# First expert stage with element 0's tokens gathered by expert, its combines beside the first retention, and weight splits over six attention pairs

## The reference, cut to what matters

```
x = x + 0.5 * ffn(layernorm(x))          # ternary weights, 1024 hidden
x = x + attention(layernorm(x))          # 16 heads of 128, rotary
x = x + 0.5 * ffn(layernorm(x))
x = x + 0.5 * moe(layernorm(x))          # first expert stage
x = x + retention(layernorm(x))
x = x + 0.5 * moe(layernorm(x))          # last expert stage

def moe(x):      # 8 experts of width 128, top 2 of softmax + bias, weights = the scores
    dw = zeros; dw[token, idx] += scores[token, idx]
    y = sum over e of dw[:, e] * ((silu(x @ W1[e].T) * (x @ W3[e].T)) @ W2[e].T)
    z = (silu(x @ Ws1.T) * (x @ Ws3.T)) @ Ws2.T      # shared expert, all tokens
    return y + z

def retention(x):
    q, k, v = xpos(x @ W_Q), xpos(x @ W_K, downscale=True), x @ W_V
    return ((q @ k.T) * decay) @ v
```

## Time and profile before

| | us |
|---|---|
| median of 3 runs | 1617.28 (1615.24 to 1617.81) |
| the profiled execution | 1616.08 |
| its span, first to last instruction | 1614.2 |
| mean granted TensorE clock | 0.997 |
| busy: TensorE, VectorE, ScalarE, GpSimd | 96%, 78%, 75%, 73% |
| first expert stage, first up to last down | 1253.1 to 1400.7 |
| last expert stage | 1491.3 to 1610.0 |

### The profile page before, as it was taken

The page is one execution under the profiler, slowest core; times in us unless marked ns, Lnnn a source line. Parts: engine busy times, 40 slices in busy tenths (PEclk is TensorE's granted clock), DMA queues, the critical chain, the costliest instruction groups (busy, mean ns, idle before and its releaser), DMA issues. The chain is left out here.

```text
span 1614.2 us, 26791 instructions
## 1 busy us (share of the span) xinstructions
PE 1556.4 (96%) x9211; PEld 904.0 (56%) x9211; DVE 1264.2 (78%) x2323; ACT 1213.3 (75%) x1904; POOL 1172.3 (73%) x823
## 2 busy tenths in 40 slices
PE   3998899999999999999999999999999999999898
PEld 2565445555555555545555555555567556688575
DVE  7888787777777777778888888778887776988628
ACT  7876888989989989888998999887665443345442
POOL 0865888888888888788888888888576322476635
PEclk9999999999999999999999999999999999999999
DMA  9312779899889888878899989977650000000532
GB/s 310 128 53 49 135 144 164 151 164 176 157 169 176 145 164 171 141 151 171 173 168 188 173 166 161 161 134 139 121 139 1 21 1 1 1 1 7 106 103 94
DMA packets 644101, 200.84 MB, mean 124 GB/s; under 512 B 601848, under 2 KB 641792, under 8 KB 643712
## 3 DMA queue, kind: packets, MB, share of 16 engines
q1 hardware_dynamic: 639392, 191.92, 60.8%
q0 software_dynamic: 1536, 4.20, 0.8%
q10 hardware_dynamic: 3040, 3.02, 0.5%
HBM read 36.91 MB, written 13.76 MB: 31 GB/s over the span
## 5 line engine op out<-in xcount | busy, mean ns | idle before, releaser
L993 POOL TENSOR_TENSOR Pl<-Pm,Ph 128x1024 f16<-128x1024 f32 x256 | 548.5, 2143 | 44.9 <-ACT Ph L1334 44.4
L1324 ACT ACTIVATE Pm<-banks,nbias,s_scale 128x1024 f32<-128x1024 f32 x256 | 307.4, 1201 | 95.7 <-DVE nbias L1953 95.3
L1951 DVE TENSOR_REDUCE nmax<-banks 128x1 f32<-128x1024 f32 x256 | 311.6, 1217 | 80.0 <-PE banks L2523 79.4
L1334 ACT ACTIVATE Ph<-Pm 128x1024 f16<-128x1024 f32 x256 | 268.1, 1047 | 1.5
L972 POOL TENSOR_TENSOR rp_b<-rp_s,rope 128x512 f32<-128x512 f32 x128 | 163.4, 1277 | 99.6 <-ACT rp_s L1301 98.0
L2521 PE MATMUL banks<-QK_hi 128*128 128x512 f16 x512 | 194.6, 380 | 2.2 <-DVE QK_lo L2051 1.6
L2522 PE MATMUL banks<-QK_lo,QK_hi 128*128 128x512 f16 x512 | 194.5, 380 | 0.0
L2523 PE MATMUL banks<-QK_hi,QK_lo 128*128 128x512 f16 x512 | 194.3, 379 | 0.0
L2523 PE MATMUL banks<-PT_hi,V_lo 128*128 128x512 f16 x512 | 194.0, 379 | 0.0
L2522 PE MATMUL banks<-PT_lo,V_hi 128*128 128x512 f16 x512 | 194.0, 379 | 0.0
L2521 PE MATMUL banks<-PT_hi,V_hi 128*128 128x512 f16 x512 | 194.0, 379 | 0.0
(11 more groups left out here) (312 smaller groups left out, 3983.8 us busy)
## 6 DMA issues: line engine op xcount, KB each, us to landing
moe_raw<-in_L_ffn_W SPq DMA_DIRECT2D x48, 128.0 KB, 2.9
w_all<-in_L_attn_w_qkv SPq DMA_DIRECT2D x3, 2048.0 KB, 15.8
a_raw<-in_L_attn_w_qkv SPq DMA_DIRECT2D x24, 256.0 KB, 3.2
PT_hi<-Ph SPq DMA_TRANSPOSE x256, 3.4
PT_lo<-Pl SPq DMA_TRANSPOSE x256, 3.4
w_rows<-m SPq DMA_DIRECT2D x9, 384.0 KB, 3.0
xs<-zeros SPq DMA_DIRECT2D x1, 2944.0 KB, 16.8
yd<-y_sb ACTq DMA_DIRECT2D x5, 512.0 KB, 2.9
```

What stands on the lines that cost most here:

```text
L993: nc.gpsimd.tensor_tensor(Pl[:, z % 4, :], Pm[:, k, :], Ph[:, z % 4, :], ALU.subtract).then_inc(pl_done.sem, 1)
L1324: nc.scalar.activation(Pm[:, k, :], two_banks[z % 2][:], ACT.Exp, bias=nbias[:, z:z + 1], scale=s_scale[:], accum_out=rsum[:, z:z + 1]).th ...
L1334: nc.scalar.activation(Ph[:, z % 4, :], Pm[:, (base * SLOTS + z) % 3, :], copy).then_inc(ph_done.sem, 1)
L1951: nc.vector.tensor_reduce(nmax[:, z:z + 1], two_banks[z % 2][:], AX, ALU.max, negate=True).then_inc(max_done.sem, 1)
```

## The change

The first expert stage gets the units of the last one, in an order of its own: shared units of element 0, shared half 0 of element 1, experts 0 and 1 on half 0 of element 1, the other shared half, six more dense units, the six gathered units (12 to 17), eight dense ones. 26 units in place of 36. Element 0's logits move into the FFN's end, its ranks and positions into the stage's beginning, scatter behind units 1 to 7, gathers behind units 20 to 25. Tiles 0 to 3 are combined behind units 22 and 23; tiles 4, 5 and 6, 7 on VectorE behind rotation groups 0 and 1 of the retention, whose second half is normalised and transposed only behind values 0 to 3. Helpers of the last stage take the stage number m and serve both. In attention the nine splits go to slots 9, 7 and 9, 9, 7 and 9, 9, 7 and 9 of pairs 9 to 14, and the scales' steps to slots 5, 8, 10 and 12 of pair 8, the rest to the second FFN.

Constants and attention:

```diff
+    FIRST_HALVES = [("d", DENSE, 0, 0), ("d", DENSE, 0, 1)]
+    FIRST_AHEAD = 8
+    UNITS = [SHARED[SORTED] + SHARED[DENSE][:1] + FIRST_HALVES + SHARED[DENSE][1:] + FIRST_ROUTED[2:FIRST_AHEAD] + TILES + FIRST_ROUTED[FIRST_AHEAD:],
+             SHARED[SORTED] + SHARED[DENSE] + ROUTED[:3] + TILES + ROUTED[3:]]
+    SCATTER_BEHIND = [{1: (0,), 2: (1, 2), **{t: (t,) for t in range(3, TT)}}, {0: (2,), 1: (3, 4), 2: (5, 6), 3: (7,)}]
+    GATHER_BEHIND = [{20: (0, 1), 21: (2, 3), 22: (4,), 23: (5,), 24: (6,), 25: (7,)},
+                     {15: (0, 1), 16: (2, 3), **{13 + t: (t,) for t in range(4, TT)}}]
+    FIRST_COMBINE_AT = {22: (0, 1), 23: (2, 3)}
+    RET_WEIGHTS_AT = (13, 15, 17)
+    FIRST_LOAD = 7
-    EXPERT_PAIRS, EXPERT_SLOTS = (9, 13), (9, 13)
+    EXPERT_SLOTS = {9: (9,), 10: (7, 9), 11: (9,), 12: (7, 9), 13: (9,), 14: (7, 9)}
```

VectorE in the second FFN and in pair 8:

```diff
+                    if f and phase == 2 and ht == 2:
+                        late_scales()
...
                 add(len(PHASES) - 2, 3)
+                if f:
+                    ln_variance(1, l + 1, 0)
...
                 mean_squares(len(PHASES) - 1)
+                if f:
+                    last_shifted(0, SORTED)
                 for j in range(TPH):
                     add(len(PHASES) - 1, j)
...
-                    if base == SCALE_PAIR and s == 7:
+                    if base == SCALE_PAIR and s == 5:
                         late_norm_maximum()
+                    if base == SCALE_PAIR and s == 8:
+                        late_norm_guarded()
+                    if base == SCALE_PAIR and s == 10:
+                        late_power()
                     if base == SCALE_PAIR and s == 12:
-                        late_scales()
+                        late_inverse()
```

TensorE (in the FFN, `if f and j == 2: router_logits(0, SORTED)` behind down 2):

```diff
+                unit_up(0, 0, experts_of)
+                unit_up(0, 1, experts_of)
+                rank_tokens(0)
+                turn(0)
+                unit_up(0, 2, experts_of)
+                unit_down(0, 0, experts_of)
+                unit_up(0, 3, experts_of)
+                turn(1)
+                unit_down(0, 1, experts_of)
+                for i in range(4, NUB):
+                    unit_up(0, i, experts_of)
+                    if i == 4:
+                        router_logits(0, DENSE)
+                    if i == FIRST_LOAD:
+                        experts_of += load_experts(0)
+                    unit_down(0, i - DOWN_LAG, experts_of)
+                for c in range(DC):
+                    if c:
+                        pe.wait_ge(mo_h_ready.sem, mo_h_ready.in_head(0, NUB - 1))
+                    transpose_part(0, l + 1, 0, c, bank[NEXT_TURN_BANK[c]])
+                for n in range(NUB - DOWN_LAG, NUB):
+                    unit_down(0, n, experts_of)
...
                 if b == 0:
-                    pe.wait_ge(x_added.sem, x_added.before(b, l) - 4)
+                    pe.wait_ge(x_added.sem, x_added.before(b, l))
                 for t in range(TPH):
                     values_of(t)
+                if b == 0:
+                    pe.wait_ge(r_vlo.sem, r_vlo.at(b, 2))
+                    transpose_x(0, l, 1, 4)
                 rotation(b, (2,))
```

VectorE's first expert stage, new (`combined_tiles` is `combine` and `ln_statistics` for each tile):

```diff
+                ln_variance(1, l, 1)
+                shifts(1, l, 0)
+                last_scores(0, SORTED)
+                last_pick(0, SORTED)
+                unit_product(0, 0)
+                last_second(0, SORTED)
+                shifts(1, l, 1)
+                unit_product(0, 1)
+                positions(0, SORTED)
+                norm_lo(0)
+                unit_product(0, 2)
+                choice_weights(0, SORTED)
+                unit_add(0, 0)
+                unit_product(0, 3)
+                norm_lo(1)
+                unit_add(0, 1)
+                for i in range(4, NUB):
+                    if i > DOWN_LAG + 2 and i != 6:
+                        unit_add(0, i - DOWN_LAG - 1)
+                    if i == 5:
+                        last_shifted(0, DENSE)
+                    if i == 6:
+                        last_scores(0, DENSE)
+                        last_pick(0, DENSE)
+                    unit_product(0, i)
+                    if i == 6:
+                        last_weights(0, DENSE)
+                        unit_add(0, i - DOWN_LAG - 1)
+                    if i in RET_WEIGHTS_AT:
+                        retention_weights_lo(RET_WEIGHTS_AT.index(i))
+                    combined_tiles(FIRST_COMBINE_AT.get(i, ()))
+                    if i == 23:
+                        ln_variance(0, l + 1, 0)
+                    if i == 24:
+                        shifts(0, l + 1, 0)
+                unit_add(0, NUB - DOWN_LAG - 1)
+                for c in range(DC):
+                    ln_lo_part(0, l + 1, 0, c, bank[NEXT_TURN_BANK[c]])
+                for n in range(NUB - DOWN_LAG, NUB):
+                    unit_add(0, n)
+                rotation(0, (0,))
+                combined_tiles((4, 5))
+                rotation(0, (1,))
+                combined_tiles((6, 7))
+                ln_variance(0, l + 1, 1)
```

GpSimd (`rows_lower(0, 0)` also behind step 6 of the FFN's last phase) and ScalarE:

```diff
+                rows_lower(0, 1)
+                rsqrt_ln(1, l, 1)
+                pool.wait_ge(xs_zero.sem, 16)
+                for i in range(NUB):
+                    expert_lo(0, i)
+                    if i == 1:
+                        rows_placed(0)
+                    if i == 24:
+                        rsqrt_ln(0, l + 1, 0)
+                    scatter(0, SCATTER_BEHIND[0].get(i, ()))
+                    gather(0, GATHER_BEHIND[0].get(i, ()))
+                rotation(0, (0,))
+                rsqrt_ln(0, l + 1, 1)
+                rotation(0, (1,))
...
+                for i in range(4, NUB):
+                    copy_out(0, i - DOWN_LAG - 1)
+                    unit_silu(0, i)
+                    unit_hi(0, i)
+                    if i == 5:
+                        router_exponential(0, DENSE)
+                    if i in RET_WEIGHTS_AT:
+                        retention_weights_hi(RET_WEIGHTS_AT.index(i))
+                    if i == NUB - 2:
+                        normalise(0, l + 1, 0)
...
                 if b == 0:
                     rotation(b, (1,))
+                    normalise(0, l, 1)
+                    ln_hi(0, l, 1, 4)
```

More of the change, by code:

```diff
@@ L394, in build_program, with combined, last_of, added_by @@
     LOGITS, RANKS = slice(D, D + TT * NE), slice(D + TT * NE, D + (2 * TT + 1) * NE)
[L396 to L416, removed]
+    N_SORTED = N_BEST + N_SECOND + N_POSITIONS + N_CHOICE
+    def combined(m, k, t):
+        return m * TOPK * TT + TOPK * t + k + 1
+    def last_of(m, b, half):
+        return max(i for i, u in enumerate(UNITS[m]) if u[0] != "x" and u[1:3] == (b, half))
+    def added_by(m, n):
+        return x_added.before(0, MOE_STAGES[m]) + 4 * sum(u[0] != "x" for u in UNITS[m][:n + 1])
+    def routed(m, b, step):
+        return m * (N_SORTED + N_BEST + N_WEIGHT) + b * N_SORTED + step
+    def lo_of_unit(m, i):
+        return lo_pool.sem, m * NUB + i + 1
+    def width(m, i):
+        kind, _, g, _ = UNITS[m][i]
         return GROUP_TILES[g] * P if kind == "x" else HALF
@@ L2215, in done @@
                     ins.then_inc(router_step.sem, 1)
-                    dve.wait_ge(router_step.sem, routed(b, step[0]))
+                    dve.wait_ge(router_step.sem, routed(m, b, step[0]))
                 return done
@@ new lines, in first_experts, with norm_lo, combined_tiles @@
+            def first_experts(l):
+                def norm_lo(half):
+                    for c in range(DC):
+                        ln_lo_part(1, l, half, c, bank[FIRST_TURN_BANK[half][c]])
+                def combined_tiles(tiles):
+                    for t in tiles:
+                        combine(0, t)
+                        ln_statistics(0, l + 1, t)
+                ln_variance(1, l, 1)
[34 more added lines that the diff above has]
+                unit_add(0, NUB - DOWN_LAG - 1)
+                for c in range(DC):
+                    ln_lo_part(0, l + 1, 0, c, bank[NEXT_TURN_BANK[c]])
[6 more added lines that the diff above has]
+                ln_variance(0, l + 1, 1)
@@ L2369, in last_experts @@
                     if i == WEIGHTS_AT:
-                        last_weights(1)
-                    product(i)
+                        last_weights(1, DENSE)
+                    unit_product(1, i)
                     if i == 1:
@@ L2381, in last_experts @@
                     for t in COMBINE_AT.get(i, ()):
-                        combine(t)
+                        combine(1, t)
                 for n in range(NUB - DOWN_LAG - 1, NUB):
-                    add(n)
+                    unit_add(1, n)
             def retention_weights_lo(part):
@@ new lines, in _, with load_experts @@
+            tile_registers = [nc.tensor.alloc_register(f"expert{j}") for j in range(SLOT_TILES)]
+            def load_experts(m):
+                pe.wait_ge(router_step.sem, routed(m, SORTED, N_BEST + N_SECOND + N_POSITIONS))
```

(3 more changed lines are left out.)

797 lines of the change are left out of this document (295 added, 502 removed).

## The result

The changed kernel takes 1626.4 us (median of four runs, 1624.7 to 1628.9) where the kernel before takes 1617.5 (median of four): the ratio is 1.0060, 95% interval 1.0048 to 1.0072. It is slower by some 9 us, beyond the 0.2% that can be told from no change. Forecast was 1621, own range 1615 to 1627, with slower as the likeliest outcome. The profiled execution took 1625.1 us, its span is 1623.3, so it stands 9.0 above the one profiled before.

The account below looks back on a forecast made before the run. The prediction took TensorE, busy 96% of the span, as the bound; work removed and stops added summed to +3.7 us on the profiled 1616.1, giving 1619.8, or 1621 against the runs' median; range 1603 to 1630, the forecast's own 1615 to 1627.

Parts of the forecast that it names:

- Work removed: First expert stage on TensorE: six gathered units replace element 0's 16 routed units; gain 31.9 us.
- 1, FFN tail: End of the FFN: TensorE's squares wait behind GpSimd's subtraction put ahead of the last sum of squares; +1.1 us.
- 3, positions: Before unit 2: TensorE waits for the low parts that stand behind positions; +4.1 us (2.5 to 5.5).
- 5, registers: Loading 23 registers on TensorE's queue, partly covered by up 7; +1.7 us (0.5 to 2.2).
- 6, scatter: 16 indirect DMAs behind units 1 to 7, done before TensorE comes to unit 12; 0 us.
- 7, stage end: From up 20's end to rotation group 0: gathers, combines, variance and normalisation hold down 22 and unit 25; +8.7 us (6 to 11).
- 8, entry: Rotation group 0 to group 2: rotations, combines and variance queue on VectorE before normalisation; +12.5 us (10 to 14).
- 9, clock: Half-clock stretches behind longer TensorE stops, two drops taken; +3.3 us (0 to 6.6).
- Attention: Parting pair 8's scales and moving splits to even pairs removes TensorE stops; -3.7 us (-5 to -1).
- first rival: VectorE not behind at rotation group 0, short combines, overlapping waits, no clock drop there; 1606 us, chance 0.28.
- The second: Rival that GpSimd's indirect DMAs and the idle clock cost more: slower combines, positions, two more drops; 1629 us, chance 0.18.
- The third: Rival that spreading splits over six pairs buys nothing, l_inv still stopping TensorE; 1625 us, chance 0.09.

Follow-up runs that it names:

- e6: Changed kernel with VectorE's add of unit 21 put ahead of the combines of tiles 2 and 3 and the first half's variance; 1.0057 of the kernel before.
- e2: Changed kernel with rotation group 1's VectorE work behind the second half's shifts, and ScalarE normalising before it rounds group 1's sums; 1.0032 of the kernel before.
- e5: Changed kernel with 48 more matmuls of 128x512, sums never read, on TensorE in the entry's 12.05 us stop; 1.0051 of the kernel before.
- e12: Changed kernel without its attention part: weight splits and late scales as in the kernel before; 1.0078 of the kernel before.
- e11: Changed kernel with reordered stage end and entry, earlier router, other split slots, and element 1's first low parts ahead of shifts and positions; 0.9933 of the kernel before.
- e3: Changed kernel with rotation group 1's work later at the entry and combines 4 and 5 moved into VectorE's pause behind product 24; 1.0019 of the kernel before.
- e8: Changed kernel with entry reordered, combines 4 and 5 and element 1's router earlier, unit 21's add ahead, even-pair splits in slots 9 and 13; 0.9966 of the kernel before.

## Why the prediction came out

The list of stops held, each at its place and behind the engine named; three sizes did not: clock, entry and attention. The sum was +3.7 on the profiled execution, +9.0 came. By its steps:

- **Work removed.** 33.7 us, not 31.9: the six gathered units took 28.7, my lower bound of 28.8, since nothing before them dropped the clock as in the earlier trace rows. The agreement that I claimed with 81 ns per pair was that of a sum which held half-clock time: here, at full clock, the pairs began 0.06 us apart in unit 12 and 0.08 to 0.09 in units 15 to 17.
- **1, FFN tail.** A stop of 0.84 us where I had 1.1. **2, ranks.** 3.48 for 3.6. **3, positions.** Transposes' start to unit 2 is 4.71 us, less 0.87 of work 3.8 for 4.1. **4, router.** 5.30 for 5.0.
- **5, registers.** Nothing: up 7's end and down 5 touch. The 2.2 us of the earlier trace rows are wholly covered by a full queue. Wrong by 1.7.
- **6, scatter.** 0, as said; the last of it was issued at 1306.6, unit 12 came at 1319.2.
- **7, stage end.** End of up 20 is 1358.00, so E = U + 34.1 where I had 33.0. The wait within down 22 was 4.57 for 3.1. e6 shows that moving this stop gains little, 1.5 us of this stretch in its trace and nothing clear in its time; the chain through combines and normalisation sets E, which is how I had added it up. The stretches at half clock show the same. From the end of this stop to E it is 12.27 us in the change, e2, e5 and e12, though up 25 between them took 4.94, 4.28, 3.38 and 3.30 us; e12's lines of the stop, of the start of down 23 and of E:

```profile
1380.00 0.39 PE L2448 MATMUL banks<-w,bT_hi 128*128 128x256 f16 x1 [4.51 <-DVE X L2224]
...
1384.55 0.27 PE L2448 MATMUL banks<-w,bT_hi 128*128 128x256 f16 x1
...
1392.27 0.38 PE L2448 MATMUL banks<-x,r_hi 128*128 128x512 f16 x1
```

- **8, entry.** 24.2 us for 21.2. The 12.06 us in front of the transposes was expected as "some 12". The transposes ran 2.71 us and 1.42 followed. VectorE ended the variance at E + 16.3 where I had 13.8. Nearly all of that is combines 4 and 5, 4.84 us for my 2.7; rotations and combines 6 and 7 took what I had. The first combine after rotation 0 took 2.53 us for its two operations, the one at 1404.75 0.99.

GpSimd's timeline beside that combine shows what ran at its side:

```profile
1397.63 2.84 POOL L1057 TENSOR_TENSOR rq_lo<-rot,rq_hi 128x512 fp32r<-128x512 f32 x2
...
1408.55 1.05 POOL L905 TENSOR_TENSOR rstd<-ve,small 128x4 f32<-128x4 f32 x1 [8.08 <-DVE ve L1640]
```

The two low parts lie over the drawn-out combines at 1396.81 and 1399.72, which took 2.53 and 1.55 us; between 1400.5 and 1408.5 GpSimd is idle, and each pair of operations took 0.99. The Trainium skill (SBUF — State Buffer, section SBUF: two separate sides) describes VectorE and GpSimd as blocking each other for a whole instruction on a port they share; the trace agrees at this place.

- **9, clock.** I took 3.3 us (0 to 6.6). Worked out from the timeline, the stretches at half clock lengthened TensorE's work by 1.3 (16 matmuls in the feed-forward part's tail), 1.1 (transposes before unit 2), 1.9 (up 2), 0.6 and 0.8 (down 4, up 7), 0.6 and 2.4 (down 22, up 25), 1.8 (transposes at the entry) and 1.8 (rotation group 2), some 12 us. Not all of it is time of the kernel. What lies beside a longer chain of other engines is covered: down 22 and up 25 by the chain to E (12.27 us whatever up 25 takes), the transposes at the entry by ScalarE (e5), those before unit 2 by VectorE, which goes from positions into the low parts at 1267.96 without a wait. An estimate of what counts is the rest, 1.3 + 1.9 + 0.6 + 0.8 + 1.8 = 6.4 us, +3.1 against my term. I had judged from the 2.36 us stop before 701.41 that a stop may go by at full clock and took two drops for four; behind all four there was one, and a fifth behind a stop of 0.84 us that I had priced as a stop alone.
- **Attention.** -1.0 us by the pairs' sum, for -3.7. The first half (the scales) was worth 3.7 and not 2.4, the second (six pairs) cost 2.65 instead of gaining 1.3. The step that failed: I took a split moved to an even pair for free and did not ask what stands behind slot 7.

Against the terms, then: clock +3.1, entry +3.0, attention +2.7, stage end +1.1; against them work removed -1.8, registers -1.7, steps 1 to 4 -0.3, steps moved into the feed-forward part -0.3, and 0.5 us less behind rotation group 2. That makes 5.3, the whole difference. It rests on one execution of each kernel, so a part of it may be chance: the half clock in the feed-forward tail, 1.3 us, is there in only three of ten executions (below). That the measured time lies inside my own range owes something to luck as well, since terms that I had too large took back 4.6 us of the 9.9 that I had too small. The ends of my bounds add up to -12 and +18, not to -11 and +17.

The first rival (1606) fell: tiles 4 to 7 were not normalised at E + 7.8 but at E + 21. e11 brings the entry to 14.1, and there gathering gains, so the rival's condition was worth looking at. The second (1629) was 2.6 us off where the forecast was 5.4, and had two of the three causes: the clock (3.3, for 3.1) and drawn-out combines (3.6, of which 2.1 came at the entry). I had held against it that only rotations run beside the entry; it was GpSimd's low parts of rotation 0 that ran beside these combines. The third (1625) was closest in time, and for its reason only half: the spread did buy nothing, the scales' parting did.

## What to carry to other kernels

When work leaves the engine that bounds, write out the queue of the next engine behind it, operation by operation, and look for what stands between the last result and the first reader: here reordering alone, no work saved, turned +9 us into -11. A stop that vanishes when one operation moves tells little (e6); one that shrinks with the whole chain (e2, e3) is the price. And time an added piece of work by the slot in which it stands, not by its length: the same two splits cost an even pair 0.05 or 0.3 us in slots 9 and 13, and 1.2 in slots 7 and 9. A stretch at half clock costs only where TensorE is what the next step waits for: here about half of some 12 us.

## What was not expected of the hardware

- The granted clock was 0.50 for nine of a group of twelve 128x512 matmuls although TensorE had been busy without a gap for 10.4 us at 1.00; between lay 5.2 us with two waits, of 1.09 and 1.41 us, and eight fp32 transposes (e5). Whether the transposes or the gaps do it was not tried.
- The stop of 0.82 to 0.85 us before the last sums of squares is followed by eight matmuls of 128x1 and 16 of 128x256. In the changed kernel and nine experiments that have this stop, these 16 ran at full clock seven times (1.96 to 1.99 us) and partly at half clock three times (the change 3.28, e2 3.18, e8 2.80). So the same stop in the same code can go by or not, and one trace doesn't tell which it will be. What decides it is open.
- The same gathered up of 48 matmuls with 128 columns took 2.9 to 3.4 us in the first three units and 4.1 to 4.2 in the fourth and fifth, in the changed kernel and in every experiment that kept the units' order, at full clock; the sixth unit's 36 went at the slow pace too, 3.1 us. What slows them is open.
- Loading 23 registers on TensorE's queue showed no wait behind up 7 here, and 2.2 us in the last stage.
